# Self queries and keys of a decoder layer reach their score stacks through DRAM, with the work beside the score pairs laid out anew

## What is computed

```python
x = _layernorm(x + _L0_attn_ref(x, wq, wk, wv))
x = _layernorm(x + _L0_xattn_ref(x, ctx, ctx, mask, Wq, bq, Wk, bk, Wv, bv, Wo, bo))
x = _layernorm(x + _L0_ffn_ref(x, router_w, router_b, w1, b1, w2, b2))
# self attention: q, k = rope(x @ wq.T), rope(x @ wk.T)
# rope: out_re = re * cos - im * sin, out_im = re * sin + im * cos, for pairs of neighbouring features
attn = softmax(q @ k.T / 4); out = attn @ (x @ wv.T)
```

## Time and profile before

| | |
|---|---|
| median of 3 runs | 2271.69 us |
| the profiled execution's own time | 2272.11 us |
| its span | 2270.4 us |
| TensorE busy (matmuls) | 2163.7 us, 95% of the span |
| VectorE, ScalarE, GpSimd busy | 1200.3, 1004.9, 601.0 us |
| mean granted TensorE clock | 0.965 of full speed |
| attention stage | to about 1650 us of the span |

### The profile page before, as it was taken

How to read it: one execution, slowest core, us unless ns; L and a number is a source line. 1 busy time by engine, 2 the same in 40 slices (tenths; PEclk the granted TensorE clock), 3 DMA queues, 4 the chain that set the end, 5 groups by cost and what they waited for, 6 DMA issues and landing times. The chain is left out here.

```text
span 2270.4 us, 48602 instructions
## 1 busy us (share of the span) xinstructions
PE 2163.7 (95%) x18846; PEld 1506.0 (66%) x18846; DVE 1200.3 (53%) x2522; ACT 1004.9 (44%) x1538; POOL 601.0 (26%) x937
## 2 busy tenths in 40 slices
PE   7899999999999999999999999999799999999990
PEld 4566666666666666666666666666478778787780
DVE  3466676766767767777677776764111111111114
ACT  1355555555555555555555555553231222212225
POOL 2113222332223322233222332222212122121223
PEclk6899999999999999999999999998799999999995
DMA  6311111211101110011000010000113332333217
GB/s 179 105 29 31 35 31 49 65 36 62 34 27 36 37 30 24 22 28 34 28 25 23 27 34 24 27 20 13 37 35 84 77 68 36 82 84 77 24 17 303
DMA packets 97666, 115.72 MB, mean 51 GB/s; under 512 B 12096, under 2 KB 91021, under 8 KB 95392
## 3 DMA queue, kind: packets, MB, share of 16 engines
q1 hardware_dynamic: 68112, 82.38, 11.7%
q0 software_dynamic: 17664, 18.35, 5.2%
q10 hardware_dynamic: 11664, 11.88, 1.8%
HBM read 64.53 MB, written 56.05 MB: 53 GB/s over the span
## 5 line engine op out<-in xcount | busy, mean ns | idle before, releaser
L867 DVE TENSOR_REDUCE smax<-ps_s 128x4 f32<-128x1024 f32 x500 | 609.3, 1219 | 311.3 <-PE ps_s L574 265.8
L753 ACT ACTIVATE prob<-ps_e 128x1024 f32<-128x1024 f32 x500 | 511.9, 1024 | 525.6 <-PE ps_e L583 403.6
L574 PE MATMUL ps_s<-stack 17*128 17x256 f32 x4000 | 573.7, 404 | 26.6 <-DVE smax L867 21.1
L583 PE MATMUL ps_e<-stack 18*128 18x256 f32 x4000 | 572.4, 404 | 6.9 <-DMA stack<-nrows 5.1
L574 PEld LDWEIGHTS ps_s<-stack 17*128 17x128 f32 x4000 | 347.8, 186 | 207.8 <-issue 115.8
L583 PEld LDWEIGHTS ps_e<-stack 18*128 18x128 f32 x4000 | 344.6, 186 | 12.2 <-DMA stack<-nrows 7.1
L1534 ACT ACTIVATE hid<-m_ps_h,b_sb 128x320 f32<-128x320 f32 x256 | 135.0, 527 | 415.5 <-PE m_ps_h L1494 415.5
L1494 PE MATMUL m_ps_h<-m_cols,w_sb 128*128 128x320 f32 x1024 | 293.1, 435 | 0.6 <-DVE m_cols L1551 0.6
L1511 PE MATMUL m_ps_o<-w_sb,hid 128*128 128x256 f32 x1280 | 278.9, 379 | 0.0
L1511 PEld LDWEIGHTS m_ps_o<-w_sb,hid 128*128 128x128 f32 x1280 | 243.2, 190 | 34.8
L599 PE MATMUL ps_w<-prob,val 128*32 128x256 f32 x4096 | 257.5, 394 | 1.7 <-ACT prob L753 1.7
(11 more groups left out here) (134 smaller groups left out, 2241.8 us busy)
## 6 DMA issues: line engine op xcount, KB each, us to landing
w_sb<-in_w SPq DMA_DIRECT2D x16, 1024.0 KB, 6.4
slot_rows_dram<-fill ACTq DMA_DIRECT2D x8, 1290.0 KB, 10.7
m_rows<-slot_rows_dram SPq DMA_DIRECT2D x16, 645.0 KB, 4.7
xT<-in_xT SPq DMA_DIRECT2D x32, 256.0 KB, 2.8
ctxT<-in_ctxT SPq DMA_DIRECT2D x32, 256.0 KB, 2.8
x_res<-in_x SPq DMA_DIRECT2D x32, 256.0 KB, 3.1
stack<-nrows SPq DMA_DIRECT2D x512, 2.0 KB
sums_dram<-x SPq DMA_DIRECT2D x32, 256.0 KB, 2.2
```

Of the source, the lines that this page charges most:

```text
L574: mm = nc.tensor.matmul(scores[:, p % 2, t, :], stack[X][rows, Q, p // HG, t * P:(t + 1) * P], stack[X][rows, K, p // HG, :], start=True, ...
L583: mm = nc.tensor.matmul(shifted[:, p % 2, t, :], stack[Y][rows, K, h // HG, t * P:(t + 1) * P], stack[Y][rows, Q, h // HG, :], start=True, ...
L753: nc.scalar.activation(prob[:, h:h + 2, :].rearrange("p h s -> p (h s)"), shifted[:, :, :, :].rearrange("p h t s -> p (h t s)"), ACT.Exp, ...
L867: nc.vector.tensor_reduce(max_columns(X, p), scores[:, :, :, :], AX.X, ALU.max)\
```

## The change

1. The columns of the self weights are reordered once by VectorE (`turn_columns`) into `turn_weights`, so that the self projection puts features on partitions: 8 matmuls of 256 columns (for Q and K, real and imaginary part, two halves of the features summed over), with the weights as the stationary side. The rotary tables are widened to the same layout once (`rope_wide`, four transposes, a copy to `rope`).
2. `turn` works on Q, then on K, in that layout; GpSimd adds (`turned_part`) into `turned`.
3. The self stacks are no longer transposed. SyncE writes `turned` to `stack_image_dram` (`write_part`: two DMAs of 128 rows of 1 KB for Q, two for K) and reads the image back as the stack (`read_half`: two DMAs of 256 KB for each half). The image's constant rows are written once at the start, by ScalarE's queue, which also does write and read for image 0.
4. SyncE's order in the CROSS slot: maxima of SELF half 1, write Q, write K, maxima of CROSS half 0, read half 0, read half 1, load of the context.
5. The side work of TensorE, VectorE and ScalarE is laid out anew between the pairs; the table of banks is written out. Queries of SELF are now projected in pair 7 of the SELF slot and pair 1 of CROSS, keys in pair 3 of CROSS; `values` stands in halves; shares and choice stand in CROSS pair 0 instead of pair 4, their gates likewise; the second mean in CROSS pair 7, behind the values.

```diff
+        uses = [("pv", SELF, 1, -1), ("max_rows", CROSS, 1, -2), ("out_rows", SELF, 0, -1), ("out_rows", SELF, 1, -1),
+                ("values", SELF, 0, 0), ("project", CROSS, 0, -1), ("x2_columns", CROSS, 0, -3), ("pv", CROSS, 0, -2),
+                ("columns", SELF, 0, -1), ("project", CROSS, 1, -1), ("max_rows", SELF, 0, 0), ("route", CROSS, 0, -3),
+                ("stack_k", CROSS, 0, -1), ("stack_q", CROSS, 0, -1), ("project", SELF, 0, 1),
+                ("pv", CROSS, 1, -2), ("max_rows", SELF, 1, 0), ("stack_k", CROSS, 1, -1), ("out_rows", CROSS, 0, -2),
+                ("out_rows", CROSS, 1, -2), ("stack_q", CROSS, 1, -1), ("project", SELF, 1, 1), ("pv", SELF, 0, 0),
+                ("max_rows", CROSS, 0, -1), ("count", CROSS, 0, -3), ("values", CROSS, 0, -1), ("columns", CROSS, 0, -2),
+                ("project_out", CROSS, 0, -2)]
...
+        def write_part(eng, b, part):
+            eng.wait_ge(turned_made.sem, turned_made.count(b, part + 1))
+            if part == 0:
+                if b > 0:
+                    for half in range(2):
+                        eng.wait_ge(stack_in[half].sem, stack_in[half].count(b - 1))
+            rows = DRAMS.image.rearrange("(j r) t c s -> j (r t) c s", j=HG)
+            for c in range(2):
+                eng.dma_start(rows[:, STRIP * c:STRIP * (c + 1), part, :], turned[:, part, c, :]).then_inc(written[part].sem, 16)
+        def read_half(eng, b, half):
+            for part in (Q, K):
+                eng.wait_ge(written[part].sem, written[part].count(b))
+            if b == 0:
+                eng.wait_ge(image_made.sem, image_made.count(0))
+            if e_mm[SELF].due(b - 1, 4 * half + 4):
+                eng.wait_ge(e_mm[SELF].sem, e_mm[SELF].count(b - 1, 4 * half + 4))
+            for part in (Q, K):
+                eng.dma_start(stack[SELF][:, part, 2 * half:2 * half + 2, :],
+                              DRAMS.image[:, 2 * half:2 * half + 2, part, :]).then_inc(stack_in[half].sem, 16)
...
+                else:
+                    if there(i + 1):
+                        write_part(sp, i + 1, Q)
+                        write_part(sp, i + 1, K)
+                    if there(bX):
+                        place_maxima(CROSS, bX, 0)
+                    if there(i + 1):
+                        read_half(sp, i + 1, 0)
+                        read_half(sp, i + 1, 1)
+                    if there(bX) and there(bX + 1):
+                        sp.wait_ge(v_mm[CROSS].sem, v_mm[CROSS].count(bX))
+                        load_src(sp, CROSS, bX + 1)
...
-                    mm = nc.tensor.matmul(out, src[SELF][:, piece, half * P:(half + 1) * P], wqk[SELF][:, piece, :],
-                                          start=(piece == 0), stop=(piece == KD - 1))
...
+                for k in range(KD):
+                    if Y == SELF:
+                        mm = nc.tensor.matmul(out[:, piece * S:(piece + 1) * S], turn_weights[:, k, half, piece, :],
+                                              src[SELF][:, k, :], start=(k == 0), stop=(k == KD - 1))
...
-                        pe.wait_ge(tr_ev[X].sem, tr_ev[X].count(bX, m // 2 + 2))
+                        if X == SELF:
+                            pe.wait_ge(stack_in[m // 4].sem, stack_in[m // 4].count(bX))
...
+            def beside_cross(i, m):
+                if m == 0 and there(i - 2):
+                    with_values(CROSS, i - 2, 1)
+                if m == 1:
+                    if there(i + 1):
+                        project(SELF, i + 1, 1)
+                    if there(i):
+                        max_rows(SELF, i, 1)
+                    if there(i - 1):
+                        make_stack("stack_k", CROSS, i - 1, 1)
+                if m == 2:
+                    if there(i - 2):
+                        out_rows(CROSS, i - 2, 0)
+                        out_rows(CROSS, i - 2, 1)
+                    if there(i - 1):
+                        make_stack("stack_q", CROSS, i - 1, 1)
+                if m == 3 and there(i + 1):
+                    project(SELF, i + 1, 2)
+                    project(SELF, i + 1, 3)
+                if m == 4 and there(i):
+                    with_values(SELF, i, 0)
+                if m == 5:
+                    if there(i - 1):
+                        max_rows(CROSS, i - 1, 0)
+                    if there(i - 3):
+                        count(i - 3)
+                    if there(i - 1):
+                        values(CROSS, i - 1, 0)
+                    if there(i - 2):
+                        columns(CROSS, i - 2)
...
+                        columns_of = wqk[SELF][:, k, part * D:(part + 1) * D]\
+                            .rearrange("p (t j c f) -> p c j f t", t=GROUPS_OF_4, j=HG, c=2)[:, c, :, :, :]
+                        nc.vector.tensor_copy(turn_weights[:, k, part, c, :].rearrange("p (j f t) -> p j f t", j=HG, f=R // 2),
+                                              columns_of).then_inc(weights_turned[part].sem, 1)
...
+            def turn(b, part):
+                dve.wait_ge(qk_mm[SELF].sem, qk_mm[SELF].count(b, part + 1))
+                if turned_made.due(b - 1, part + 1):
+                    dve.wait_ge(turned_made.sem, turned_made.count(b - 1, part + 1))
+                pair = work("project", SELF, part).rearrange("p (c s) -> p c s", c=2)
+                cos = rope[:, 0, :].unsqueeze(1).to_broadcast([P, 2, S])
+                nc.vector.tensor_tensor(qk[:, part, :, :], pair, cos, ALU.mult).then_inc(qk_ev[SELF].sem, 1)
+                nc.vector.scalar_tensor_tensor(rot[:, part, 0, :], pair[:, 1, :], -1.0, rope[:, 1, :], ALU.mult, ALU.mult)\
                   .then_inc(qk_ev[SELF].sem, 1)
...
+            def beside_cross(i, m):
+                if m == 0 and there(i - 3):
+                    shares(i - 3)
+                    choose(i - 3)
+                if m == 1 and there(i + 1):
+                    turn(i + 1, Q)
+                if m == 2 and there(i - 2):
+                    divide(CROSS, i - 2, 0)
+                    divide(CROSS, i - 2, 1)
+                if m == 3 and there(i + 1):
+                    turn(i + 1, K)
...
+                if m == 6 and there(i - 2):
+                    second_sum(i - 2)
+                if m == 7:
+                    if there(i - 1):
+                        values(CROSS, i - 1)
+                    if there(i - 2):
+                        mean_and_variance(CROSS, i - 2, 5, y2, stats2)
+                    if there(i - 3):
+                        own_positions(i - 3)
...
+            def turned_part(b, part):
+                if b > 0:
+                    pool.wait_ge(written[part].sem, written[part].count(b - 1))
+                pool.wait_ge(qk_ev[SELF].sem, qk_ev[SELF].count(b, 3 * (part + 1)))
+                ready()
+                nc.gpsimd.tensor_tensor(turned[:, part, :, :], qk[:, part, :, :], rot[:, part, :, :], ALU.add)\
+                  .then_inc(turned_made.sem, 1)
```

439 lines of the change are left out of this document (216 added, 223 removed).

## The result

The change makes the kernel slower: 2306.77 us (median of 4 runs, 2302.42 to 2312.17) against 2270.77 beside it; the ratio is 1.0165, with a 95% interval of 1.0132 to 1.0198. The prediction was 2245, with a range of 2204 to 2278.

A forecast was written before the change was run, and what follows sets the result against it. TensorE was taken to bound the attention stage. Transposes -73.9, the maxima wait -12, two new waits +51 and the start +8 sum to -26.9 from 2272.1 profiled, giving 2245 us, range 2204 to 2278.

The forecast's parts named there:

- The start, +8: Before the first score: reordering weights and tables, and image 0's write and read, cost 8 us; bounds 5 and 15.
- The image's transfers, half 0 landing 3.7 us after its issue: Before pair 0 of a SELF slot: TensorE waits 1.0 us a loop for the image's read; bounds 0 and 3.7.
- New wait 1: At CROSS's output rows: TensorE waits 0.65 us a loop for a bank that VectorE's turn reads; bounds 0 and 1.2.
- VectorE's 0.41 us should go: Before a pair of score heads: TensorE's wait for VectorE's maxima vanishes in some 29 full loops, -12 us.
- Transposes -2.31: Self stacks: four groups of four transposes per image leave TensorE, 2.31 us an image, -73.9 us over 32 images.
- what stays equal: Self projection in 8 matmuls of 256 columns, values in halves, turn and addition: no change, the projection within 0.1 us.
- The tail: End of the kernel, behind the last full loops: the prediction's sum had no term for it.
- (b): Rival: the image's write uses a quarter of the DMA engines, 0.3 to 0.6 us a loop; 2262 us, chance 0.15.
- T: Reference time in the image's chain: TensorE's start of the maxima's transpose in CROSS pair 5; read issue forecast about 4.0 us later.
- (c): Rival: slower than before, the read of half 0 lands over 1.0 us later and bounds the loop; 2329 us, chance 0.13.
- (d): Rival: VectorE takes the gain back, maxima late in pairs with the turn; 2267 to 2277 us, chance 0.05.
- (a): Rival: one or both new waits stay away, TensorE the only bound; 2194, or 2214 to 2225 us, chance 0.25.

The follow-up runs named there:

- e1: Changed kernel with ScalarE's nine large DRAM fills moved to the self stages of steps 1 and 2; 2372.73 us, ratio 0.9717 to the kernel before, stalled series.
- e8: e6 plus the DRAM fills moved later and 18 warming matmuls ahead of the last self columns; 2267.47 us, ratio 0.9995 to the kernel before.
- e6: Changed kernel with the image's write over 32 outer rows and half 0's read issued before the maxima's transfers; 2275.22 us, ratio 1.0029 to the kernel before.
- e14: Changed kernel with only the image's write spread over 32 outer DRAM rows instead of 4; 2375.89 us, ratio 0.9749 to the kernel before, stalled series.
- e13: Control: the changed kernel again with no edit; 2390.09 us, ratio 0.9806 to the kernel before, stalled series.
- e11: e6 with the second norm's statistics in the last cross pair taking 32 of 256 columns; 2334.56 us, ratio 0.9567 to the kernel before, stalled series.
- e7: Changed kernel with the values made whole again, self in pair 3 and cross in pair 7; 2354.02 us, ratio 1.0383 to the kernel before.
- e16: e8 plus warming matmuls ahead of the waits for images 0 and 1; 2364.52 us, ratio 0.9695 to the kernel before, stalled series.
- e15: Changed kernel with only half 0's read issued ahead of the maxima's transfers; 2450.49 us, ratio 1.0058 to the kernel before, stalled series.

## Why the prediction was wrong

It said 26.9 us less; the profiled executions differ by 40.0 more. The steps that failed are the start (+8, measured +27.6), the work taken from TensorE (-2.31 us a loop, measured -1.40), the landing of the read (3.7 us, later by 1 to 2 in seven steps of 25, with a clock that had no price), and a tail without a term. The gap of 66.9 by the prediction's own steps:

- **The start, +8: measured +27.6 at the first landmark.** This term missed by 19.6. The first score at 28.04 us lay in the forecast's 22 to 30, and 12.6 later than before, inside the term's bounds of 5 to 15; the other 15 come behind it. What I left out was image 1, whose write and read meet ScalarE's fills, and the clock, which is lower behind the two standstills. I priced only the chain of image 0, and bounded it by that. Taking the fills away gives 7 to 11 us back (e1, e8 against e6), the write over 32 rows with them on the order of 12 (e14 against e13), and with both the start is still 1 to 6 us behind that of the kernel before.
- **"The image's transfers, half 0 landing 3.7 us after its issue": right in the short steps, missed in the long ones.** The wait's mean was the forecast 1.0 us (26.0 us in 25), at the place and with the issue time forecast, but that mean is luck: 17 waits of 0.5 to 0.8 and seven of 1.7 to 2.6, in which the same read lands 4.5 to 5.5 us after its issue. The long steps cost 19 us in 27: about 10 are the longer waits themselves, the rest the lower clock behind four of them. I had named the clock among what would prove me wrong (it is 0.97 in 850 to 900 us), and had given it no price. e6, without these waits, has no step over 47.3 in the steady part.
- **New wait 1, 0.65 us: measured 0.20** (the rot row). In its place came two that I did not have, 0.25 for ScalarE's stack copy and 0.26 for VectorE's maxima. All waits in a short step are 1.30 us, against 1.65 forecast; with the long ones they are 44.0 us in 1200, some 1.7 a step, which is near the forecast by luck.
- **"VectorE's 0.41 us should go": it did not.** 6.6 us in 25 steps remain, and with the image's wait gone 19.0 (e6), some 0.75 a step. The premise was false: "a score pair finds its maxima done two pairs back". It needs those of the pair right before it, since all pairs share `ps_s`. Where TensorE has less work between two pairs than the maxima take with their two hand-overs, it waits, whatever else VectorE has to do (e11).
- **Transposes -2.31 and "what stays equal" 0 a loop: together the miss of the short step.** It fell by 0.51 us where the forecast was 1.03 to 1.07. From TensorE's timeline of 500 to 1300 us, in the steps of ordinary length, each piece counted from its start to the next start less the wait between: TensorE's work is 47.02 us a step before and 45.62 after, 1.40 less and not 2.31, while the waits go from 0.41 to 1.30. Transposes 4.28 to 2.19, so 2.09 and not 2.31; the self projection 3.73 to 3.92 in pieces of 256 columns; the values 3.74 to 4.01 in halves; the output projection 1.83 to 1.93; the transposes of normalised rows 1.08 to 1.19; the last tenths are spread over the others. Moving a piece or cutting it in two was not free. I guessed after the result that the halved values cost it; they have 0.2 to 0.3 us of it, but with the values whole the step is longer (e7).
- **The tail: the sum leaves about -7 for it, measured +7.6.** It had no term of its own. TensorE waits 4.2 us there for the self normalisation of the last image, at a place without warming matmuls, and half clock follows. e8 gives back 5.6.
- **Rivals.** (b), four DMA engines, is right as a mechanism (e16 against e15: 2.2 us of landing; a quarter of the engines at work), but K's write landed at T+3.7, ahead of the read's turn and not behind it, so it cost nothing there alone; it was priced at 14 us of steps and 3 of start, and alone is worth about 5 and 12 (e14 against e13). (c) asked for a read that lands 4.7 us after its issue in each step; in seven of 25 it took 4.5 to 5.5, so (c) has its mechanism in those steps, and the rest of the slower result came by other roads. (d) is right in part: VectorE's maxima stand behind the image. (a) is wrong.

Start, long steps and tail make about 19.6 + 19 + 14 of the 67, the short step another 14. In each the step that failed is the same in kind: I summed a steady step, with its pieces at their old lengths, and left its two ends and the steps that come out long unpriced.

What stays open: why the read lands 1 to 2 us later in seven of 25 steps, and why the lower clock follows only four of these waits.

## What to carry to other kernels

Price a new DRAM round trip where the pipeline is not yet full, with the traffic that is in flight then, and give the tail a term of its own. When a wait is removed, list what else ends at the same pair before crediting its length: here the image, VectorE's maxima and their transfers ended within half a microsecond, and the read had two bounds 0.3 us apart, so one edit alone gave 14 us or cost 60 (beside stalls), and the two together 34 (without). Where all pairs share one tile, give TensorE between two pairs at least as much other work as the reading of that tile takes with its hand-overs; that was worth more than 1 us a step here (e7).
